# Layer 4 of a fused decoder kernel: scores on 32 rows, values on 32 columns, exponentials from the bank

## The reference

```python
def _L1_xattn_ref(q, k, v, gamma):
    B, Dq, Lq = q.shape            # 8, 128, 256
    h = 8
    dq = Dq // h                   # 16
    qh = q.reshape(B, h, dq, Lq)
    kh = k.reshape(B, h, dq, Lk)   # Lk = 256
    vh = v.reshape(B, h, dv, Lk)
    qk = jnp.einsum('bhdq,bhdl->bhql', qh, kh) * scale    # scale = 1/4
    sm = jax.nn.softmax(qk, axis=-1)
    ret = jnp.einsum('bhql,bhdl->bhdq', sm, vh)
    return gamma * ret.reshape(B, Dv, Lq)
...
x = _layernorm(x + _L1_xattn_ref(x, ctx_2048, ctx_2048, L1_xattn_gamma), axis=-1)
```

## Time and profile before

| | |
|---|---|
| time, median of 3 runs | 2314.27 us (2311.66 to 2315.75) |
| the profiled execution | 2315.22 us |
| its span, first to last instruction | 2313.4 us |
| instructions | 30622 |
| mean granted clock of TensorE | 0.931 |
| TensorE busy | 2037.0 us, 88% of the span |
| VectorE, ScalarE, POOL busy | 1354.1, 1056.5, 643.6 us |

### The profile page before, as it was taken

How to read it: one execution, slowest core, us unless ns; L and a number is a source line. 1 busy time by engine, 2 the same in 40 slices (tenths; PEclk the granted TensorE clock), 3 DMA queues, 4 the chain that set the end, 5 groups by cost and what they waited for, 6 DMA issues and landing times.

```text
span 2313.4 us, 30622 instructions
## 1 busy us (share of the span) xinstructions
PE 2037.0 (88%) x11200; PEld 1604.5 (69%) x11200; DVE 1354.1 (59%) x2885; ACT 1056.5 (46%) x2391; POOL 643.6 (28%) x645
## 2 busy tenths in 40 slices
PE   7999778896898897899899999898599988999887
PEld 6887456775777776577788888466488854555576
DVE  3555455654566667776444444548644456888766
ACT  3333255652444444444233333166333338888432
POOL 1212100001232323321122221344322223788422
PEclk9999879997999999899899999988699989999989
DMA  4000420002001000000243323000032310000011
GB/s 192 24 24 1 118 56 1 1 13 109 1 1 37 35 5 31 35 1 1 68 132 98 118 106 114 0 1 1 35 104 95 100 37 34 1 1 1 1 47 46
DMA packets 25242, 105.60 MB, mean 46 GB/s; under 512 B 3258, under 2 KB 9146, under 8 KB 21124
## 3 DMA queue, kind: packets, MB, share of 16 engines
q1 hardware_dynamic: 24260, 103.25, 13.1%
q10 hardware_dynamic: 832, 0.39, 0.1%
HBM read 97.56 MB, written 6.07 MB: 45 GB/s over the span
## 4 chain that ended last, share of the span: by engine, by line
PE 46%; DVE 5%; ACT 4%; issue 2%; POOL 2%; DMA 0%; POOLq 0%; DVEq 0%; SPq 0%
PE ps L145 41%; PE ps L262 5%; ACT AR L148 2%; DVE AR L151 1%; POOL AR L151 1%; DVE stt L325 1%; DVE AR L162 1%; DVE X L156 1%; DVE Y L151 1%; ACT L148 0%; ACT CR L2807 0%; ACT R L1915 0%; POOL R L151 0%; DVE AR L2387 0%; POOL rs L151 0%
## 5 line engine op out<-in xcount | busy, mean ns | idle before, releaser
L145 PE MATMUL ps<-R 128*128 128x512 f32 (+2 forms) x4944 | 912.0, 343 | 71.1 <-POOL R L151 48.0
L145 PEld LDWEIGHTS ps<-R 128*128 128x128 f32 (+1 forms) x4944 | 777.1, 194 | 194.7 <-issue 44.2
L148 ACT ACTIVATE AR<-AR 128x128 f32<-128x128 f32 (+4 forms) x681 | 337.4, 558 | 288.7 <-DVE AR L151 173.0
L145 PE MATMUL ps<-AR 128*128 128x17 f32 (+4 forms) x2496 | 363.2, 296 | 16.2 <-DVE AR L151 7.6
L145 PEld LDWEIGHTS ps<-AR 128*128 128x128 f32 (+2 forms) x2496 | 302.0, 180 | 77.0 <-issue 50.8
L151 POOL TENSOR_TENSOR R<-W,R 128x768 fp32r<-128x768 f32 (+2 forms) x110 | 180.7, 1653 | 576.0 <-ACT R L1889 496.1
L151 DVE TENSOR_TENSOR AR<-ps,AR 128x512 f32<-128x512 f32 (+2 forms) x358 | 201.3, 576 | 229.4 <-PE ps L145 216.8
L262 PEld LDWEIGHTS ps<-cf,AR 128*128 128x128 f32 (+3 forms) x1376 | 172.2, 150 | 174.3 <-issue 70.0
L262 PE MATMUL ps<-cf,AR 128*128 128x128 f32 (+3 forms) x1376 | 227.7, 285 | 74.0 <-DVE AR L151 16.8
L151 POOL TENSOR_TENSOR AR<-AR 128x512 f32<-128x512 f32 (+2 forms) x124 | 126.7, 1022 | 380.7 <-DVE AR L151 212.3
L1915 ACT CAST R<-AR 128x512 fp32r<-128x512 f32 x148 | 92.0, 622 | 302.2 <-DVE AR L151 292.4
(11 more groups left out here) (174 smaller groups left out, 2059.2 us busy)
## 6 DMA issues: line engine op xcount, KB each, us to landing
W<-in_wts SPq DMA_DIRECT2D x14, 1920.0 KB, 8.4
AR<-shd SPq DMA_DIRECT2D x32, 512.0 KB, 3.6
W<-in_wts SPq DMA_DIRECT2D x4, 2048.0 KB, 8.6
AR<-shd SPq DMA_DIRECT2D x20, 384.0 KB, 3.5
W<-in_wts SPq DMA_DIRECT2D x5, 1280.0 KB, 7.5
AR<-shd SPq DMA_DIRECT2D x20, 256.0 KB, 3.9
W<-in_wts SPq DMA_DIRECT2D x2, 1536.0 KB, 7.7
AR<-shd SPq DMA_DIRECT2D x20, 128.0 KB, 3.8
```

The source lines that it names most:

```text
L145: return self.e.matmul(o, l, r, start=start, stop=stop, skip_group_check=True)
L148: return self.e.activation(o, i, f, bias=bias, scale=scale)
```

## The change

It touches `ColumnAttention` alone.

- `KB` is 128x512: the context twice, multiplied by `par`, a mask of the even and of the odd head of each pair. VectorE makes `par` from `bm16` when the layer starts. The product of a pair of heads takes 32 rows of `X` and of `KB`.
- The loop of TensorE goes over 32 pairs of steps v. In one: two score products on neighbouring 32 rows into two of the banks 0 to 3, a part of the value products of an earlier batch, then the eight transposes of the pair of steps before.
- VectorE only takes the maximum, negated. ScalarE exponentiates from the bank with it as the bias, one head at a time.
- The values are the weights (`VZ`, 32 columns for a pair of heads, with zeros for the other head), the exponentials move, 256 queries at a time, and the output of pair hp stands on the rows 32 hp to 32 hp + 31 of bank 6, already upright. A second set of products with ones (`OZ`) gives the sums for each of these rows. A batch has 8 such groups of 4 products, made in three parts of 3, 3 and 2 groups.
- `P` now holds a whole batch. ScalarE copies bank 6 to `OS` (`lifted`); VectorE takes the reciprocal of 256 columns, multiplies with the output and gamma, and adds the state.

```diff
             def pe(self, e):
                 ...
+                for v in range(39):
+                    if v < 32:
+                        b, r = divmod(2 * v, 8)
+                        qc, hp = divmod(r, 4)
                         need_x(e, l, b)
                         e.wait_ge(*T.keyed.at(b + 1))
-                        e.wait_ge(*T.softed.at(i - 2))
-                        e.mm(banks[i % 3], X[:, b, tok(qc)], self.KB[b % 2][:, four(hp)], True, True).then_inc(T.scored.sem, 1)
...
+                        e.wait_ge(*T.exped.at(2 * v - 2))
+                        for x in range(2):
+                            s = slice(32 * (hp + x), 32 * (hp + x + 1))
+                            t = e.mm(banks[(2 * v + x) % 4], X[s, b, tok(qc)], self.KB[b % 2][s, :], True, True)
+                        t.then_inc(T.scored.sem, 1)
+                    if v == 33:
+                        self.pe_values(e, 7, range(8))
+                    elif 5 <= v < 33 and v % 4 != 0:
+                        self.pe_values(e, (v - 5) // 4, (range(3), range(3, 6), range(6, 8))[(v - 5) % 4])
+                    if 1 <= v <= 32:
+                        e.wait_ge(*T.copied.at(2 * v - 2))
+                        for x in range(2):
+                            e.wait_ge(*T.exped.at(2 * v - 1 + x))
+                            t = pe_turn(e, self.E[(2 * v - 2 + x) % 4], banks[4 + x])
+                        t.then_inc(T.turned.sem, 1)
+                    if v % 4 == 2 and v >= 10:
+                        pe_turn_state(e, l, v // 4 - 2)

+            def pe_values(self, e, b, part):
+                T, O, P = self.T, banks[6], self.pairs(b)
+                e.wait_ge(*T.copied.at(8 * b + 8))
+                e.wait_ge(*T.vplaced.at(b + 1))
+                e.wait_ge(*T.lifted.at(b))
+                for k in part:
+                    kind, h, c = k // 4, k // 2 % 2, k % 2
+                    for hp in range(4):
+                        left = self.OZ[:, 32 * h:32 * (h + 1)] if kind == 0 else self.values(b)[:, c, h, 32 * hp:32 * (hp + 1)]
+                        t = e.mm(O[32 * hp:32 * (hp + 1), 256 * kind:256 * (kind + 1)], left, P[:, hp, h, c, :], k % 4 == 0,
+                                 k % 4 == 3)

             def dve(self, e):
+                e.red(self.par, cfc("bm16").rearrange("p (n h) -> p h n", h=2), ALU.add).then_inc(T.parity.sem, 1)
+                for i in range(75):
+                    b = i // 8 - 2
+                    if i % 8 == 0 and 0 <= b:
+                        OS = self.OS[b % 2]
+                        e.wait_ge(*T.lifted.at(b + 1))
+                        e.e.reciprocal(OS[:, 0:256], OS[:, 0:256]).then_inc(e.sem, e.up())
                         e.settle()
+                        e.st3(OS[:, 256:512], OS[:, 256:512], smc("gam"), OS[:, 0:256], ALU.mult, ALU.mult).then_inc(T.shared.sem, 1)
+                        e.wait_ge(*T.shared.at(b + 1))
+                        dve_add(e, l, b, OS[:, 256:512])
+                    if i % 8 == 2 and 0 <= b:
                         dve_norm(e, l, b)
                     if i < 64:
-                        e.wait_ge(*T.scored.at(i + 1))
-                        e.wait_ge(*T.turned.at(i - 3))
-                        dve_soft(e, banks[i % 3], self.E[i % 4], self.m[i % 4], 2, 256, T.softed)
+                        e.wait_ge(*T.scored.at(i // 2 + 1))
+                        e.wait_ge(*T.exped.at(i - 3))
+                        e.red(self.m[i % 4][:, 0:2], banks[i % 4].rearrange("p (h w) -> p h w", h=2), ALU.max,
+                              negate=True).then_inc(T.maxed.sem, 1)

             def act(self, e):
+                for v in range(39):
+                    if v % 4 == 0 and v >= 8:
+                        b = v // 4 - 2
+                        e.wait_ge(*T.valued.at(b + 1))
+                        e.wait_ge(*N[l].added.at(b - 1))
+                        e.e.copy(self.OS[b % 2], banks[6]).then_inc(T.lifted.sem, 1)
+                    if v < 32:
+                        for i in (2 * v, 2 * v + 1):
+                            e.wait_ge(*T.maxed.at(i + 1))
+                            e.wait_ge(*T.turned.at(i // 2 - 1))
+                            for h in range(2):
+                                s = slice(256 * h, 256 * (h + 1))
+                                t = e.act(self.E[i % 4][:, s], banks[i % 4][:, s], ACT.Exp, bias=self.m[i % 4][:, h:h + 1])
+                            t.then_inc(T.exped.sem, 1)
+                    if 1 <= v <= 32:
+                        for x in range(2):
+                            j = 2 * v - 2 + x
...
+                            e.wait_ge(*T.turned.at(v))
+                            e.wait_ge(*T.valued.at(b - 1))
+                            e.e.copy(self.pairs(b)[:, hp].rearrange("p h c (q n) -> p (h c) q n", q=2)[:, :, qc, :],
+                                     banks[4 + x].rearrange("p (s n) -> p s n", s=4)).then_inc(T.copied.sem, 1)

             def pool(self, e):
                 e.wait_ge(s_y, 32)
+                e.wait_ge(*T.parity.at(1))
...
+                        e.tt(self.KB[b % 2].rearrange("p (h n) -> p h n", h=2),
+                             CX[:, b, :].unsqueeze(1).broadcast_to([128, 2, 256]),
+                             self.par.unsqueeze(2).broadcast_to([128, 2, 256]), ALU.mult).then_inc(T.keyed.sem, 1)
```

More of the change, by code:

```diff
@@ L1567, in __init__, with values, pairs @@
                 room = plain()
-                self.KB = room.ring(2, 2048)
-                self.v4 = room.take(2 * 64 * 17).rearrange("p (c b e) -> p c b e", c=2, b=64)
-                self.E, self.P = room.ring(4, 512), room.ring(3, 512)
-                self.m = room.ring(4, 4)
-                self.rc, self.ox = room.ring(2, 16), room.ring(2, 256)
-                self.T = stage(ones=1, vplaced=2, keyed=8, scored=64, softed=64, exped=64, turned=64, copied=64, valued=64,
-                               divided=8, upright=8)
+                self.P = room.ring(2, 4096)
+                self.KB = room.ring(2, 512)
+                self.VZ = room.ring(2, 512)
+                self.OZ = room.take(64)
+                self.par = room.take(2)
+                self.E, self.OS = room.ring(4, 512), room.ring(2, 512)
+                self.m = room.ring(4, 4)
+                self.T = stage(parity=1, zeroed=3, ones=2, vplaced=8, keyed=8, scored=32, maxed=64, exped=64, turned=32,
+                               copied=64, valued=8, lifted=8, shared=8)
+            def values(self, b):
+                return self.VZ[b % 2].rearrange("p (c h n) -> p c h n", c=2, h=2)
+            def pairs(self, b):
+                return self.P[b % 2].rearrange("p (s h c n) -> p s h c n", s=4, h=2, c=2)
+            def pe_values(self, e, b, part):
[9 more added lines that the diff above has]
+                                 k % 4 == 3)
+                if part[-1] == 7:
+                    t.then_inc(T.valued.sem, 1)
             def pe(self, e):
@@ L1618, in dve @@
                 need_room(e, l)
[L1619 to L1625, removed]
-                        e.settle()
[L1627 to L1635, removed]
+                e.red(self.par, cfc("bm16").rearrange("p (n h) -> p h n", h=2), ALU.add).then_inc(T.parity.sem, 1)
@@ L1642, in act @@
             def act(self, e):
                 T, l = self.T, self.l
[L1644 to L1657, removed]
+                for v in range(39):
[15 more added lines that the diff above has]
+                            j = 2 * v - 2 + x
+                            b, r = divmod(j, 8)
+                            qc, hp = divmod(r, 4)
[3 more added lines that the diff above has]
+                                     banks[4 + x].rearrange("p (s n) -> p s n", s=4)).then_inc(T.copied.sem, 1)
+                    if v % 4 == 2 and v >= 10:
+                        act_copy_state(e, l, v // 4 - 2)
@@ L1661, in pool @@
                 need_room(e, l)
[L1662 to L1667, removed]
+                e.wait_ge(s_y, 32)
+                e.wait_ge(*T.parity.at(1))
+                for b in range(9):
+                    if b < 8:
+                        e.wait_ge(*T.scored.at(4 * (b - 1)))
+                        e.tt(self.KB[b % 2].rearrange("p (h n) -> p h n", h=2),
+                             CX[:, b, :].unsqueeze(1).broadcast_to([128, 2, 256]),
+                             self.par.unsqueeze(2).broadcast_to([128, 2, 256]), ALU.mult).then_inc(T.keyed.sem, 1)
+                    if b == 0:
+                        for x in range(2):
+                            e.e.memset(self.VZ[x], 0.0).then_inc(T.zeroed.sem, 1)
+                        e.e.memset(self.OZ, 0.0).then_inc(T.zeroed.sem, 1)
+                        e.wait_ge(*T.zeroed.at(3))
+                        for h in range(2):
+                            e.e.memset(self.OZ[:, 48 * h:48 * h + 16], 1.0).then_inc(T.ones.sem, 1)
+                        e.wait_ge(*T.ones.at(2))
+                    if b < 8:
```

(8 more changed lines are left out.)

## The result

| | before | after |
|---|---|---|
| time, median of 6 runs | 2315.01 us (2311.66 to 2317.95) | 2326.61 us (2322.39 to 2328.84) |
| profiled execution, its span | 2315.22, 2313.4 us | 2322.39, 2320.6 us |
| mean granted clock | 0.931 | 0.920 |

The changed kernel is slower: the ratio is 1.0048, with a 95% interval of 1.0035 to 1.0062. That is 11.6 us; forecast were 11.

A forecast was written before the change was run, and what follows sets the result against it. TensorE was taken to bound layer 4 now, 18.0 us a batch. Afterwards a 17.9 us cycle through all engines saves 9.0, the start adds 3.4 (net -5.6), the clock adds 17: +11, 2326 us; range 2305 to 2368.

The forecast's parts named there:

- the mechanism: Layer 4, each batch: TensorE's saved 5.3 us becomes idle time behind VectorE's block, and the idle lowers the clock, +11 us.
- the rivals: Three alternatives for layer 4: clock holds (chance 0.20), value columns run two at a time (0.20), columns don't overlap (0.12).
- the clock did not hold: Denied rival, TensorE's idle 5 us a batch: the clock stays full, giving 2309 us, or 2304; chance 0.20.
- value columns ran four at a time: Forecast 0.43 us a value part; rivals: two at a time, 0.86, 2353 us, chance 0.20; no overlap, 1.71, 2408, 0.12.
- TensorE's prices: Layer 4, a batch: scores 3.4, transposes 3.4, values 3.4, changes of shape 2.2, state 0.2, sum 12.7 us against 18.0.
- The step that had no row at all: TensorE's value parts: four products on different columns overlap fully, 0.43 us a part, with 1.71 as the other end.
- The prediction's argument against that rule from layer 3: Under strict order layer 3's eight records need five turns of 0.107 us, not four; the row is nearer four.
- The wait: Each batch: ScalarE idles about 4 us for VectorE's block and maximum, TensorE 5.0 us for copies; cycle 17.9 us.
- The clock's price in a cycle: After TensorE's idle 5 us, half clock costs 1.6 to 3.3 us a cycle; 2.3 taken, seven cycles 16.
- The clock while filling and at the end: Layer 4: 23.1 us to the first lift, 6.5 between the last two lifts, 1 us of clock for the first batch.
- The start: Start of layer 4: POOL waits for par behind layer 10's mask, first maximum at 943.6 instead of 940.24, +3.4 us.
- That mask ends at 940.15: Start of layer 4: layer 10's mask end, from which par, POOL's multiply and scores were summed to 943.6.

The follow-up runs named there:

- Experiment 1: Kernel after, with VectorE's block moved from before a batch's first maximum to behind its second, and the norm two steps later: 2286.26 us, ratio 0.9867.
- experiment 3: Kernel after, with the two value-product loops exchanged, so a part's products on one column group follow each other before the next group's: 2344.49 us, one run.
- experiment 2: Kernel after, with five unused 128x512 products ahead of the first value part of each batch but the first: 2311.25 us, ratio 0.9983.
- experiment 8: Kernel after, with VectorE's block later, par before the mask, POOL's multiply held back, and three unused products before the first scores: 2277.03 us, ratio 0.9863.
- experiment 4: Kernel before, with POOL's first multiply waiting for VectorE's mask of layer 10: 2307.99 us, ratio 0.9975.
- 7: Kernel after, with VectorE's block later, par made before layer 10's mask, and POOL's next multiply held back until VectorE's norm: 2283.96 us, ratio 0.9886.

## Why the prediction was right, and where only its sum was

The time was foreseen within 1 us, the mechanism was the one named, and the rivals fell: the clock did not hold (0.84), value columns ran four at a time, and VectorE's block in its place made TensorE wait. But two terms were off by some 6 us each and cancelled, so the hit within 1 us is luck; that a stall and the clock behind it turn the saving into a loss was foreseen.

- **TensorE's prices held.** Value parts of three products a group at full clock: 1016.75 to 1018.19 less the change of shape, 1.3 us, so 0.43 for four products; score pairs 0.86; changes of shape 0.2. Experiment 1, where TensorE pauses for only 1.2 us a batch, has 12.54 us of it busy, predicted 12.7. The step that had no row at all, 0.43 for four columns and not 1.71, was a choice with 0.43 as its best end; it came true, and experiment 3 shows that it hangs on the order of the loop. By the rule of strict order, from the Trainium skill's page "TensorE: Matmul & The Clock Gate", Part 3, it would have been 0.86 (an estimate); the kernel after shows 0.43. The prediction's argument against that rule from layer 3 was weak: by its own count of one load and n times 0.107 us, four turns give 0.54 us and five give 0.64, and the row has 0.65. What decides is the kernel after: the value parts, and a score pair that with its change of shape takes 1.06 us, where records in strict order would need three times 0.43, 1.28.
- **The wait held.** Predicted: ScalarE idle about 4 us, TensorE 5.0, cycle 17.9 at the full clock. Measured: 4.07, 4.93, and 17.75 with the clock held up in experiment 2.
- **The clock's price in a cycle held**: 2.3 predicted, 2.6 measured (20.37 - 17.75).
- **The clock while filling and at the end was mis-sized.** Predicted: 23.1 us from the first maximum to the first lift, and 1 for the clock. Measured: 29.05 (the first lift starts at 963.23, the first maximum at 934.18). The granted clock was 0.50 from the first scores on until about 954.7. In experiment 8, where it is at 1.00 from 935 us on, it is 23.7 (the first reciprocal starts at 957.55, 0.65 behind the lift, and the first maximum at 933.18), so 5.3 us are the clock's, not 1. At the end the eight value parts took 5.28 us with half of their records at the half clock, and the last two lifts were 8.4 us apart in place of 6.5; in experiment 1 the last two reciprocals are 6.75 us apart and the clock is 1.00, so 1.6 are the clock's.
- **The start was wrong in sign.** Predicted +3.4 us, measured 6.60 - 9.65 = -3.05. The failing step is "That mask ends at 940.15": it took the mask's end of the kernel before for that of the kernel after. The mask was late there because POOL's two multiplies, 7.78 us, ran beside it and held VectorE up. The change makes POOL wait until the mask is done, which the prediction itself says, and experiment 4 shows that this wait alone brings the mask's operations to 0.69 us. The prediction took POOL's shorter multiply as "otherwise hidden" and never asked why a cast of 1024 columns should take 4.09 us.

So, by parts: start -3.05, and from the first maximum to the end 166.3 us against 152.5, +13.8; together +10.75, which is the layer's 10.8. Of the 166.3, 15.7 (six cycles at 2.62) + 5.3 + 1.6 = 22.6 are the clock's. At the full clock that leaves 143.7, predicted 143.5. The clock was 5.6 us more than the forecast's 17, the start 6.5 less than forecast.

What stays open: how far TensorE looks ahead (experiment 3, one run), why the clock at the layer's end was full in experiments 1 and 7 and half in 8, and why layers with the same code differ by up to 7 us between executions of different kernels.

## What to carry to other kernels

An engine's order is part of the change's price. Ask of each long block that stands once in a loop whether the next engine's only work waits behind it, and put it after the operations that feed that engine: here two steps were worth 41.5 us. When another engine's work shrinks or moves, look for instructions beside it that were far longer than their size, since they too will move. And price an idle TensorE twice, once for the wait and once for the clock behind it: 4.93 us of waiting cost 2.6 us more.

## What the runs showed of the hardware that was not expected

- Four f32 products on four column groups of 32, with 256 moving columns, take 0.43 us together when issued one from each group in turn. With three in a row from each group they took twice as long, with two in a row they didn't (experiment 3).
- A VectorE cast to 128x1024 f32 and a two-constant operation of that size took 0.69 us each, and 4.09 and 3.97 each beside a POOL multiply of 3.9 us; a norm of 128x256 took 0.41, and 1.02 beside a POOL multiply of 1.04.
- Five unused products in an idle time of 4.9 us made the kernel after some 15 us faster (2326.6 to 2311.3; layer 4 by 14.4), by the clock alone.
